# Border rows written to memory in three parts and read back by one transfer per half: a two-stage depthwise convolution stack

## The reference

```python
x = x + _L0_conv_ref(_gn(x), w1, w3, w5, alpha)   # stage X
x = x + _L1_conv_ref(_gn(x), w, b)                # stage Y
```

## Time and profile before

| | us |
|---|---|
| median of three runs (lowest to highest) | 431.48 (428.29 to 431.5) |
| the profiled execution, its own time | 432.64 |
| its span, which the rows count in | 430.8 |
| PE / DVE / ACT / POOL busy in the span | 318.5 / 318.1 / 304.1 / 262.3 |

### The profile page before, as it was taken

The page is one execution under the profiler, slowest core; times in us unless marked ns, Lnnn a source line. Parts: engine busy times, 40 slices in busy tenths (PEclk is TensorE's granted clock), DMA queues, the critical chain, the costliest instruction groups (busy, mean ns, idle before and its releaser), DMA issues.

```text
span 430.8 us, 12547 instructions
## 1 busy us (share of the span) xinstructions
PE 318.5 (74%) x5206; PEld 276.8 (64%) x5206; DVE 318.1 (74%) x688; ACT 304.1 (71%) x372; POOL 262.3 (61%) x206
## 2 busy tenths in 40 slices
PE   2491586754986998679894998499848989898440
PEld 2361273643986798459883897389836989897220
DVE  7861899971886998399929994889649996779620
ACT  1407257089999699939995899759993999977320
POOL 6405055058788578827885588738882788865601
PEclk9997596995999899969996999889998999999685
DMA  6689488201687769676986788676868514731965
GB/s 151 169 174 204 129 188 169 73 3 41 159 200 164 199 177 210 158 189 202 199 194 171 198 184 202 161 214 173 189 163 223 145 41 118 201 97 28 264 173 146
DMA packets 112829, 69.40 MB, mean 161 GB/s; under 512 B 4540, under 2 KB 109892, under 8 KB 112772
## 3 DMA queue, kind: packets, MB, share of 16 engines
q1 hardware_dynamic: 106088, 65.31, 60.5%
q10 hardware_dynamic: 6684, 3.29, 3.3%
HBM read 41.10 MB, written 27.48 MB: 159 GB/s over the span
## 4 chain that ended last, share of the span: by engine, by line
DVE 33%; DMA 21%; SPq 13%; ACT 13%; PE 9%; issue 4%; ACTq 2%; POOL 2%; POOLq 0%; DVEq 0%
DVE xt L697 15%; DVE stats L641 13%; DMA xt<-in_x_dram 10%; PE ps L377 8%; DMA edge_scratch<-gnX 6%; ACT gn_f L551 5%; SPq L236 5%; ACT gnX L552 4%; ACT cross L561 3%; SPq L216 3%; DMA edge_scratch<-gnY 2%; SPq L250 2%; POOL gnX L864 1%; SPq L263 1%; ACTq L244 1%
## 5 line engine op out<-in xcount | busy, mean ns | idle before, releaser
L377 PE MATMUL ps<-gnX,band 64*64 64x512 f16 x2880 | 181.6, 397 | 29.9 <-DVE xt L697 18.1
L377 PEld LDWEIGHTS ps<-gnX,band 64*64 64x64 f16 x2880 | 161.1, 188 | 46.6 <-issue 40.2
L697 DVE SCALAR_TENSOR_TENSOR xt<-ps,unscale,xt 128x512 f32<-128x512 f32 (+1 forms) x194 | 143.8, 747 | 22.9 <-PE ps L377 20.1
L641 DVE BATCH_NORM_STATS2 stats<-xt 128x6 f32<-128x384 f32 x256 | 120.9, 546 | 45.6 <-DMA xt<-in_x_dram 44.9
L377 PE MATMUL ps<-gnY,band 64*64 64x512 f16 x1728 | 116.8, 414 | 33.7 <-DVE xt L697 33.7
L864 POOL TENSOR_TENSOR gnX<-gn_f,gnX 128x768 f16<-128x768 f32 x60 | 92.7, 1545 | 60.7 <-ACT gnX L552 60.7
L377 PEld LDWEIGHTS ps<-gnY,band 64*64 64x64 f16 x1728 | 97.9, 190 | 49.1 <-ACT gnY L552 23.0
L551 ACT ACTIVATE gn_f<-xt,g_add,g_mul 128x768 f32<-128x768 f32 x120 | 122.1, 1017 | 4.9 <-DVE g_add L681 4.3
L864 POOL TENSOR_TENSOR gnY<-gn_f,gnY 128x768 f16<-128x768 f32 x60 | 92.7, 1545 | 31.0 <-ACT gnY L552 31.0
L561 ACT ACTIVATE cross<-ps,unscale 64x512 f32<-64x512 f32 x94 | 64.2, 683 | 51.0 <-PE ps L377 49.4
L873 POOL TENSOR_TENSOR xt<-xt,cross 128x512 f32<-128x512 f32 x47 | 61.7, 1315 | 57.3 <-ACT cross L561 57.2
(11 more groups left out here) (78 smaller groups left out, 97.9 us busy)
## 6 DMA issues: line engine op xcount, KB each, us to landing
out_dram<-xt SPq DMA_DIRECT2D x56, 384.0 KB, 4.8
xt<-in_x_dram SPq DMA_DIRECT2D x48, 384.0 KB, 6.4
band<-diag_scratch SPq DMA_DIRECT2D x48, 160.0 KB, 3.0
haloX<-edge_scratch SPq DMA_DIRECT2D x32, 123.4 KB
xt<-in_x_dram SPq DMA_DIRECT2D x20, 192.0 KB, 4.3
xt<-in_x_dram ACTq DMA_DIRECT2D x12, 192.0 KB, 6.0
out_dram<-xt SPq DMA_DIRECT2D x12, 192.0 KB, 4.0
haloX<-edge_scratch SPq DMA_DIRECT2D x32, 61.7 KB
```

Source lines behind the costliest of these rows:

```text
L377: mm = nc.tensor.matmul(ps[to, c, half, :], weights(rows, half), moving(rows, half), start=first, stop=last)
L641: st = nc.vector.bn_stats(stats[:, q_of(at, i) % 2, at, b, e, :], flat[:, SUB * e:SUB * (e + 1)])
L697: ev = nc.vector.scalar_tensor_tensor(out=here, in0=ps[frm, c, half, :].rearrange("h (b w) -> h b w", b=NB), scalar=unscale[rows, at:at + ...
```

## The change

`edge_dram` gets a third part that holds the high rows once more. `edges_out` writes it with an extra transfer beside each of the old ones (in X 8 transfers per unit instead of 4, in Y 4 instead of 2). `edges_in` then reads all three parts with one transfer per set of partitions (2 per unit instead of 4). What arrives in the halo is the same. The counts that the semaphores are compared with follow.

```diff
-        edge_dram = [nc.dram_tensor(f"edge_scratch{s}", [2, 2, 2, 2, FAR[s], ROW], fp16, kind="Internal").ap() for s in (X, Y)]
+        edge_dram = [nc.dram_tensor(f"edge_scratch{s}", [2, 2, 3, 2, FAR[s], ROW], fp16, kind="Internal").ap() for s in (X, Y)]
...
-            return 64 * (n // 2 + 1)
+            return 32 * (n // 2 + 1)
...
-                        eng.dma_start(edge_dram[s][p, g, :, side, :, :].rearrange("h r e -> r h e"), src).then_inc(edges_landed[s], 16)
+                        eng.dma_start(edge_dram[s][p, g, 0:2, side, :, :].rearrange("h r e -> r h e"), src).then_inc(edges_landed[s], 16)
+                        eng.dma_start(edge_dram[s][p, g, 2, side, :, :], src[:, 0, :]).then_inc(edges_landed[s], 16)
...
-                    eng.dma_start(edge_dram[s][p, :, :, side, 0, :],
+                    eng.dma_start(edge_dram[s][p, :, 0:2, side, 0, :],
                                   bass.AP(src.tensor, src.offset, [[R * pitch, 2], [2 * ROW, 2], [1, ROW]]))\
                        .then_inc(edges_landed[s], 16)
+                    eng.dma_start(edge_dram[s][p, :, 2, side, 0, :],
+                                  bass.AP(src.tensor, src.offset, [[R * pitch, 2], [1, ROW]])).then_inc(edges_landed[s], 16)
...
-            n = rows * len(taps)
-            eng.wait_ge(edges_landed[s], (64, 32)[s] * (i + 1))
+            n = 3 * rows * len(taps)
+            eng.wait_ge(edges_landed[s], (128, 64)[s] * (i + 1))
...
-                for at, parts in ((0, 2), (2, 1)):
-                    eng.dma_start(halo[s][R * g + at * n:R * g + (at + parts) * n, p, :, :, :]
-                                  .rearrange("r b c w -> r (b c w)")[:, 0:EDGE],
-                                  bass.AP(src.tensor, src.offset + taps[0], [[ROW, parts * rows], [1, len(taps)], [1, EDGE]]))\
-                       .then_inc(halo_in[s][p], 16)
+                eng.dma_start(halo[s][R * g:R * g + n, p, :, :, :].rearrange("r b c w -> r (b c w)")[:, 0:EDGE],
+                              bass.AP(src.tensor, src.offset + taps[0], [[ROW, 3 * rows], [1, len(taps)], [1, EDGE]]))\
+                   .then_inc(halo_in[s][p], 16)
```

## The result

The changed kernel takes 425.01 us (median of 4 runs, 420.72 to 425.71) against 429.88 us of the kernel before (4 runs: the three named under "Time and profile before" and one of 427.72). The ratio is 0.9851, with a 95% interval of 0.9802 to 0.9901: 1.5% faster, 6.4 us by the ratio; the two medians by themselves lie 4.9 us apart. 423.0 us was forecast. The profiled execution took 425.71 us, its span is 423.9 us. It lies near its kernel's median; the profiled execution of the kernel before (432.64) lies 2.8 us above its own, so of a difference between these two traces some 2 to 3 us can be the spread of executions.

What follows compares the result with a forecast made beforehand. Bound by SP's edge transfers and the late load DVE awaits in odd periods: five times -1.6 is -8.0, long SP stretch -0.6, end +0.1, sum -8.5 us; 432.64 to 424.1, beside the median 423.0 us (chance 0.38), range 415.5 to 433.

Steps and rivals of the forecast that it cites:

- What bounds the kernel: In five odd periods DVE waits 4.56 to 8.03 us for a load that SP issues late, behind `edges_out` and `edges_in`.
- (a): `edges_out` of X, odd periods: four more transfers, +1.2 us of issuing, mostly covered by the landing; +0.5 us taken.
- (b): `edges_in` of X, odd periods: two of four issues go, on the path; -1.4 us each period.
- Size adds little: `edges_in` of X: the larger issue takes nearly the same time, as 123.4 and 61.7 KB took 0.73 and 0.66 us.
- (c): Landing of image 3 of the load, odd periods: less time behind the halo's transfers; -0.7 us, bounds -1.4 and +1.4.
- (e): Exchanges where engines hold the chain: X +1.2 and -1.4, Y +1.1 and -1.3 us on SP, a wash.
- (d): Chain on SP from 173 to 208 us, two Y exchanges and one X: -0.6 us, bounds -3 and +4.
- (f): The end, on ACT's queue: two more outs, two fewer ins; +0.1 us, bounds -2 and +2.
- the slower rival: At a full queue each added transfer pays, 0.6 to 0.83 us in X, up to 1.35 in Y: 437.5 us, chance 0.14.
- The rival of few engines: The halo is slow because its transfers run on few DMA engines, and 60 rows use more: 417 us, chance 0.24.
- a window near 0.7: A DMA share near 0.7 in the halo window, 0.44 before, would show that few engines carried the halo.
- The rival that the load is bound by the DMA engines: Image 3 lands when its queue is empty, whenever issued: about -1 us in all, 430.5 us, chance 0.24.

Runs made afterwards that it cites:

- the writes alone: Changed kernel with `edges_in` back at four transfers, the second of each half reading the third part: 450.49 us, ratio 1.0477 against the kernel before.
- the reads alone: Changed kernel with the third part written for the first two units alone, so later units read old data: 407.81 us, ratio 0.9486 against the kernel before.
- the Y-only kernel: The change made in stage Y alone, X left as in the kernel before: 430.69 us, ratio 1.0016 against the kernel before.
- the four wide issues: Changed kernel with each `edges_in` transfer cut in two along the row, same partitions, four issues again: 451.41 us, ratio 1.0519 against the kernel before.
- The two narrow issues: Changed kernel with the taps outermost in the source of `edges_in`, so border rows come out wrong: 448.58 us, ratio 1.0444 against the kernel before.

## Why the prediction was right or wrong

The forecast was right, and in the main for its reason: the gain lies on the path on which it was looked for, from SP's edge transfers over the load to DVE, and nowhere else in the stretch (85.0 to 77.8 us against 115.1 and 115.4). It was 1.45 us per odd period, where 1.6 was forecast. That the sum came so near was partly luck, as its three terms were each off and made up for one another. It is also no tool for the parts of the change: by the same terms, added up, the writes alone would have been forecast at some 6.5 us more and the reads alone at some 15 less (an estimate), and they were +20 and -22.

- **What bounds the kernel.** Right: SP, the edges' landing and the load in the odd periods, the engines between. What it did not see is that SP issues for 159 of the 185 us, so that it is ahead by next to nothing in the rest.
- **(a), added writes in odd periods, +0.5.** Mis-sized: `edges_out` +0.57, landing wait -0.71, together -0.14. The issues cost 1.2, but 0.6 less was lost at a full queue. Why there was more room was not separated, and the trace of the Y-only kernel, whose `edges_out` of X is that of before, also has 1.52 us where the kernel before has 2.02.
- **(b), two issues fewer, -1.4.** Measured -1.11. The issue that replaces two takes 0.82 us, not 0.66. "Size adds little" misled here: the two of 123.4 and 61.7 KB differ by little (0.65 and 0.61 for the second pair), and yet the whole takes 0.82.
- **(c), the load's landing, -0.7.** Measured -0.19. That few engines carry the halo can't be read from the half-empty window of before, which the four wide issues have too. The two narrow issues show that the spread can matter (+2.3 us at this very landing when it is made narrower than the changed kernel's).
- **(e), "The other exchanges ... cost nothing while SP stays ahead of its next wait".** It held for the change, since issuing of 159.2 and 160.4 us is the wash that (e) speaks of, and the engine parts stayed as they were. It held by a narrow margin: SP is hardly ahead, and every kernel here that issues 18 us more or beyond in the stretch pays for it there. Its second sentence, that the terms of (d) would then hold for the others too, comes near what the writes-only kernel shows: 3.5 us more in each engine part, and the writes' share in the terms of (d) is 1.8 + 0.3 + 1.4 = 3.5.
- **(d) and (f)**, small terms, weren't tested by themselves. In even periods the eight issues took 4.0 us on average where the four of before took 3.0: they do not pay the full queue each, as the slower rival had it. Of the eight, the first two or three are slowed and the others take 0.26, so it was room that was lacking, as argued. In the changed kernel's slowest such exchange, on SP's timeline:

```profile
139.21 1.31 SPq L216 DMA_DIRECT2D edge_scratch<-gnX  x1
140.58 1.33 SPq L217 DMA_DIRECT2D edge_scratch<-gnX  x1
141.96 0.26 SPq L216 DMA_DIRECT2D edge_scratch<-gnX  x1
142.26 0.27 SPq L217 DMA_DIRECT2D edge_scratch<-gnX  x1
```

That rival named the right place for what more issuing would cost (SP at each exchange), at too high a price: the added issues cost about their plain 0.30 and 0.56 us.
- **The rival of few engines** (417 us): its sign, a window near 0.7, came (0.68), and its time did not; the window also fills because the load is issued earlier, as the four wide issues show. **The rival that the load is bound by the DMA engines** (430.5 us) has fallen: the load, issued earlier, took no longer to the statistics (7.54 and 7.35), and DVE's waits shrank by 6.7 us.

## What to carry to other kernels

When one queue issues nearly all DMAs, sum its issue times over a steady period before looking at the chain, and note how long after its data was ready each exchange starts. If issuing fills most of the period and the exchanges start just in time, the price of a transfer has two sides: one more costs nearly its issue time wherever it stands, since the queue falls behind everywhere, while one less pays only on the part of the period whose chain runs over the queue. A merge that adds as many issues as it takes away can still gain, if those it takes away stand on that part and those added stand in a wait for a landing. So price the two sides apart, part by part, and put long issues (a load) into the waits of a round trip. Look at the outermost dimension of a small transfer too: the same bytes in the same two issues cost 23 us more when it went from 12 and 6 to 5 and 3.

## What the runs showed of the hardware

The issue of one transfer on SP, with room in its queue, took 0.26 us (two neighbouring partitions, one or two rows each), 0.40 (one run of 16 bytes), 0.46 to 0.56 (two partitions 64 apart), 0.59 to 0.73 (halo transfers of 6 to 40 partitions), 0.79 (18) and 0.82 us (60 partitions). I had not expected two rows to be cheaper than 16 bytes, nor the two-partition transfers to differ by a factor of two. It isn't the number of partitions alone: the transfer of 18 in the changed Y took longer than one of 20 or 40 in the old X; what sets it was not looked at. The Trainium skill (page "DMA: Bandwidth & Descriptors", section "Issuing engines are not separate DMA queues") says that issuing from several engines only saves the time to initiate, "which is usually small relative to the DMA itself"; small it is, yet here SP's issuing fills 86% of the stretch, and 62 transfers of 16 bytes, four in a period, cost 14 us. In this kernel that sentence misleads.
